# Attention heads' output turned to feature rows by DMA, and the first unit's score maxima computed twice

## What is computed

```python
x = x + 0.5 * ffn0(layernorm(x))      # (W + B @ A) scaled per output: 512 -> 512
x = x + attn0(layernorm(x))           # 32 query heads of 16, 8 key/value heads, rotary, causal
x = x + 0.5 * ffn0(layernorm(x))
x = x + 0.5 * moe(layernorm(x))       # base 512 -> 512, router over 8 experts, top 2, rank-16 LoRA
x = x + attn1(layernorm(x))           # 8 heads of 32, softmax over keys, causal
x = x + 0.5 * moe(layernorm(x))
# attention: softmax(q k^T * scale + causal) v, heads side by side, then @ w_o.T + b_o
```

## Time and profile before

| | |
|---|---|
| Median of three runs | 1358.18 us |
| The profiled execution's own time | 1344.81 us |
| Its span, first to last instruction | 1343.1 us |
| Mean granted TensorE clock | 0.928 of full |
| Busy: PE, DVE, ACT, POOL | 1205.7, 953.5, 671.2, 375.2 us |
| First sequence: A0's first score, its last value product ended | 116.19, 357.79 us |
| Second sequence, the same last value product ended | 1020.49 us |

### The profile page before, as it was taken

One profiled execution on the slowest core, in us unless ns is written; L12 is line 12 of the kernel. 1 busy time (PEld: TensorE's weight loads), 2 busy tenths in 40 slices (PEclk: granted clock), 3 DMA queues, 4 the chain that ended last, 5 costly groups with the idle time before them and its releaser, 6 DMA issues.

```text
span 1343.1 us, 21792 instructions
## 1 busy us (share of the span) xinstructions
PE 1205.7 (90%) x6800; PEld 753.2 (56%) x6800; DVE 953.5 (71%) x2990; ACT 671.2 (50%) x1023; POOL 375.2 (28%) x505
## 2 busy tenths in 40 slices
PE   4998999999899877998879999999988988879988
PEld 1875444443388865444868744444435887744368
DVE  5889889898166676653659798999962667576365
ACT  2621666666655452544436036666665554435542
POOL 0431411122254400114614323122213542002162
PEclk9996899999999997999979858999999999869999
DMA  8374411220010020100140742112200100120001
GB/s 317 120 196 87 125 29 26 57 65 3 1 49 1 1 47 19 55 2 0 63 175 23 189 130 70 26 26 57 66 2 0 50 1 17 32 72 2 1 8 56
DMA packets 37285, 76.20 MB, mean 57 GB/s; under 512 B 5084, under 2 KB 6620, under 8 KB 37036
## 3 DMA queue, kind: packets, MB, share of 16 engines
q1 hardware_dynamic: 37176, 74.82, 19.2%
HBM read 48.98 MB, written 27.08 MB: 57 GB/s over the span
## 4 chain that ended last, share of the span: by engine, by line
PE 64%; DVE 19%; issue 5%; POOL 5%; ACT 5%; DMA 1%; DVEq 0%; SPq 0%; ACTq 0%; POOLq 0%
PE bank L999 16%; PE bank L871 12%; PE bank L779 5%; PE bank L780 5%; PE bank L781 5%; DVE maxes L1208 5%; PE bank L983 4%; PE bank L977 3%; DVE unused L1204 3%; PE bank L765 3%; DVE ops L1152 3%; PE bank L881 2%; POOL x L1484 2%; POOL w_odd L1466 2%; ACT ops L1356 2%
## 5 line engine op out<-in xcount | busy, mean ns | idle before, releaser
L1431 ACT ACTIVATE probs<-bank 128x1024 f32<-128x1024 f32 (+3 forms) x416 | 367.9, 911 | 320.4 <-PE bank L983 220.3
L871 PE MATMUL bank<-ops 48*128 48x512 f32 (+3 forms) x960 | 321.8, 436 | 34.5 <-DVE maxes L1204 17.2
L1204 DVE CUSTOM_DVE_ANT_0 unused<-bank,causal 128x128 bf16<-128x128 f32 (+3 forms) x640 | 279.5, 486 | 47.7 <-PE bank L871 44.1
L1542 POOL TENSOR_SCALAR_AFFINE_SELECT probs<-probs 128x256 f32<-128x256 f32 (+1 forms) x256 | 118.8, 464 | 640.3 <-ACT probs L1431 640.0
L871 PEld LDWEIGHTS bank<-ops 48*128 48x128 f32 (+1 forms) x960 | 163.0, 206 | 218.9 <-DVE maxes L1204 96.0
L999 PE MATMUL bank<-probs,v_mem 128*17 128x512 f32 (+6 forms) x1920 | 252.2, 517 | 6.1 <-ACT heads_raw L1418 5.6
L1208 DVE TENSOR_REDUCE maxes<-bank 128x1 f32<-128x512 f32 x320 | 207.4, 684 | 40.7 <-PE bank L871 39.2
L983 PE MATMUL bank<-ops 50*128 50x512 f32 (+2 forms) x640 | 175.9, 448 | 5.0 <-ACT probs L1431 4.8
L779 PE MATMUL bank<-ops,xT 128*128 128x512 f32 (+1 forms) x288 | 116.2, 403 | 19.6 <-DVE x L1068 11.6
L983 PEld LDWEIGHTS bank<-ops 50*128 50x128 f32 x640 | 86.6, 197 | 57.9 <-ACT probs L1431 29.5
L1473 POOL TENSOR_TENSOR rstd<-var_eps,minus_half 128x1 f32<-128x1 f32 x96 | 52.7, 549 | 215.1 <-DVE var_eps L1046 214.5
(11 more groups left out here) (117 smaller groups left out, 1965.5 us busy)
## 6 DMA issues: line engine op xcount, KB each, us to landing
query_rows_dram<-ops SPq DMA_DIRECT2D x48, 256.0 KB, 3.8
ops<-query_rows_dram SPq DMA_DIRECT2D x64, 192.0 KB, 4.4
w_odd<-staging_wqkv SPq DMA_DIRECT2D x4, 1536.0 KB, 7.3
x<-x_dram SPq DMA_DIRECT2D x16, 256.0 KB, 6.1
ops<-ops SPq DMA_DIRECT2D x16, 256.0 KB, 3.0
out_dram<-x SPq DMA_DIRECT2D x16, 256.0 KB, 2.0
staging_wqkv<-wqkv_dram SPq DMA_DIRECT2D x2, 1536.0 KB, 15.8
key_rows_dram<-ops SPq DMA_DIRECT2D x24, 128.0 KB
```

The costliest lines, as they stand in the source:

```text
L871: last = mm(dst[:, h * w:(h + 1) * w], queries(a, u)[rows, t // 4, hi, t % 4 * P:(t % 4 + 1) * P], keys(a, u, hi)[rows, HALF * kp:HALF * k ...
L1204: V.tensor_tensor_reduce(unused[:, masked % 3, 0:w], part, causal[:, HALF - w:], 1.0, NEG, ALU.add, ALU.max, dst).then_inc(s["max_done"].s ...
L1431: A.activation(probs[:, e % 6, :, 0:cols], scores[:, 2 * (e % 2):2 * (e % 2) + 2, 0:cols], ACT.Exp, scale=a.scale).then_inc(s["exp"].sem, 1)
L1542: G.affine_select(out=p, in_=p, compare_op=ALU.is_ge, fill=0.0, base=0, pattern=pattern, channel_multiplier=-1).then_inc(s["masked"].sem, 1)
```

## The change

1. The "norm" items leave the ring, and WO0 and WO1 lose `turn_x`, `copy_turned` and `turned_lo`. Instead SP stores a chunk's raw heads (256 KB) to a DRAM scratch and loads them back twice, as rows of features with tokens along the free dimension: the values (`head_in`, 128 KB a unit and chunk) and the sum, repeated for each feature of its head (`head_sum`, 128 KB). Two units fill 128 partitions. DVE then takes the reciprocal of the sums (128x512, `inverse_sums`), POOL multiplies and splits into high and low parts (`heads_out`), and the WO products read these (`heads_T`). For the last pair of units DVE does all of it (`last_heads`): chunk 0 at the end of the attention, chunk 1 in tick 3 of the next chain.
2. In the first four steps, and in the ring's items ahead of them from the first not begun in the QKV chain, each score product of a "max" item is issued twice into the same place (`sparse`).
3. `xT` moves into `ops`; MOE_A's weights are loaded after WO0 and split in ticks of tiles 4 to 7 of FFN_B instead of 2 to 5.

```diff
-                if slot == 0:
-                    for c in range(2):
-                        e = s - self.lag - 2 - self.last_step[c]
-                        if e >= 0 and e % ns == 0 and e // ns < self.units:
-                            dst.append(("norm", e // ns, c))
...
+            def load_heads(b, st, u, c):
+                a, s = ATT[st], qs[st]
+                lanes = slice(64 * (u % 2), 64 * (u % 2) + 64)
+                sp.wait_ge(s["raw"].sem, s["raw"].at(b, 2 * u + c + 1))
+                wait(sp, s["staged"][c], b, 32 * u)
+                sp.dma_start(raw_rows[c], heads_raw[:, c, :]).then_inc(s["dumped"][c].sem, 16)
+                sp.wait_ge(s["dumped"][c].sem, s["dumped"][c].at(b, 16 * (u + 1)))
...
+                rows = raw_rows[c].rearrange("(h r) s -> h r s", r=a.head_rows)
+                sp.dma_start(head_in[lanes, c, :], rows[:, 0:a.dim, :]).then_inc(s["staged"][c].sem, 16)
+                sp.dma_start(head_sum[lanes, c, :], rows[:, a.dim:a.dim + 1, :].to_broadcast([a.unit_heads, a.dim, HALF])
+                             ).then_inc(s["staged"][c].sem, 16)
...
                     if u + 1 < a.units:
                         load_shifts(b, QKV0, u + 1, 0)
+                    load_heads(b, QKV0, u, 0)
+                    if u + 1 < a.units:
                         load_shifts(b, QKV0, u + 1, 1)
                     if u + 3 < a.units:
                         sp.wait_ge(s["scored"].sem, s["scored"].at(b, (u + 1) * a.unit_events))
                         load_queries(b, u + 3, 0)
                         load_queries(b, u + 3, 1)
-                    if u in (3, 4):
-                        load_weights(b, FFN_B if u == 3 else MOE_A)
+                    if u == 3:
+                        load_weights(b, FFN_B)
+                    load_heads(b, QKV0, u, 1)
...
                 after(b, WO0)
+                load_weights(b, MOE_A)
...
             def begin(b, st, t):
                 n = product_no(st, t)
-                pe.wait_ge(xT_ready.sem, xT_ready.at(b, TURN_NO[st, t] + 1))
+                if st in WO_ATT:
+                    a, s = WO_ATT[st], qs[QKV0 if st == WO0 else QKV1]
+                    pe.wait_ge(s["out"].sem, s["out"].at(b, 3 * (a.units - 2)))
+                    pe.wait_ge(s["last"].sem, s["last"].at(b, 3 * (t // 4 + 1)))
...
-                    for h, (r, hi) in enumerate(heads_in):
+                    sparse = max(a.begun.values()) <= i < len(a.ring_first) + sum(len(slot) for step in a.ring_at[:4] for slot in step)
+                    for h, (r, hi) in list(enumerate(heads_in)) * (2 if sparse else 1):
...
+                    if c > 0 and i == 3:
+                        last_heads(b, QKV0 if c == 1 else QKV1, 1)
                     if before is not None:
                         epilogue(b, *before)
...
+            def inverse_sums(b, st, k, c):
+                a, s = ATT[st], qs[st]
+                dve.wait_ge(s["staged"][c].sem, s["staged"][c].at(b, 32 * (2 * k + 2)))
+                V.reciprocal(head_sum[:, c, :], head_sum[:, c, :]).then_inc(s["inverse"].sem, 1)
+
+            def last_heads(b, st, c):
...
+                inverse_sums(b, st, k, c)
+                hi, lo = (heads_T(a, part, k)[:, HALF * c:HALF * (c + 1)] for part in range(2))
...
+                V.tensor_tensor(head_out[:, c, :], head_in[:, c, :], head_sum[:, c, :], ALU.mult).then_inc(s["last"].sem, 1)
+                V.tensor_copy(hi, head_out[:, c, :]).then_inc(s["last"].sem, 1)
+                V.tensor_tensor(lo, head_out[:, c, :], hi.bitcast(F32), ALU.subtract).then_inc(s["last"].sem, 1)
...
++                    for i in range(ring_no, upto):
+                        ring_read(b, st, i)
+                    ring_no = upto
+                    u, k_ = divmod(g, len(a.steps))
+                    if u % 2 == 0 and 0 < u < a.units and k_ in (2, 6):
+                        inverse_sums(b, st, u // 2 - 1, k_ // 6)
+                last_heads(b, st, 0)
...
+                        first = 4 if nst == MOE_A else 2
+                        if nb < BATCH and nst not in WO_ATT and first <= t < first + chunks_of[nst]:
+                            split_chunk(nb, nst, t - first)
...
+            def heads_out(b, st, k, c):
...
+                pool.wait_ge(s["inverse"].sem, s["inverse"].at(b, 2 * k + c + 1))
+                G.tensor_tensor(head_out[:, c, :], head_in[:, c, :], head_sum[:, c, :], ALU.mult).then_inc(s["out"].sem, 1)
+                G.tensor_copy(hi, head_out[:, c, :]).then_inc(s["out"].sem, 1)
+                G.tensor_tensor(lo, head_out[:, c, :], hi.bitcast(F32), ALU.subtract).then_inc(s["out"].sem, 1)
...
+                    if u % 2 == 0 and u > 0 and k_ in (4, 7):
+                        heads_out(b, st, u // 2 - 1, k_ // 7)
```

More of the change, by code:

```diff
@@ L411, in all_keys, with heads_T @@
             return ops_flat[:, 16384:20480] if a is A0 else ops_flat[:, 12288:20480]
+        def heads_T(a, part, k):
+            first = ((4096, 5120, 6144, 7168), (8192, 9216, 21504, 14336)) if a is A0 else ((1024, 3072), (4096, 5120))
+            return ops_flat[:, first[part][k]:first[part][k] + SEQ]
         def values(a):
@@ L505, in build @@
             s["raw"] = signal(f"{n}_heads_raw", a.chunks)
-            s["inv"] = signal(f"{n}_inverse_sum", a.chunks)
-            s["normed"] = signal(f"{n}_heads_ready", a.chunks)
+            s["dumped"] = [signal(f"{n}_heads_dumped{c}", 16 * a.units) for c in range(2)]
+            s["staged"] = [signal(f"{n}_heads_staged{c}", 32 * a.units) for c in range(2)]
+            s["inverse"] = signal(f"{n}_inverse_sums", a.units)
+            s["out"] = signal(f"{n}_heads_divided_high_low", 3 * (a.units - 2))
+            s["last"] = signal(f"{n}_last_heads_divided_high_low", 3 * 2)
             qs[st] = s
@@ L830, in product @@
                     pe.wait_ge(w_ready.sem, w_ready.at(b, chunks_before(st + 1)))
-                three_passes(prod[n % 2][:, 0, :], n, weights(st, 0), weights(st, 1)).then_inc(prod_ready.sem, 1)
+                if st in WO_ATT:
+                    x_in = ([heads_T(WO_ATT[st], part, k)[:, t * P:(t + 1) * P] for k in range(chunks_of[st])] for part in range(2))
+                else:
+                    x_in = ([xT[:, n % 2, part, k, :] for k in range(KC)] for part in range(2))
+                three_passes(prod[n % 2][:, 0, :], *x_in, weights(st, 0), weights(st, 1)).then_inc(prod_ready.sem, 1)
             def expert_half(b, st, t, first, between=None):
@@ L838, in expert_half @@
                 cols = slice(0, MOE_HALF) if first else slice(MOE_HALF, MOE_COLS)
-                last = three_passes(prod[n % 2][:, 1 if first else 0, 0:MOE_HALF], n, weights(st, 0)[:, :, cols],
+                x_in = ([xT[:, n % 2, part, k, :] for k in range(KC)] for part in range(2))
+                last = three_passes(prod[n % 2][:, 1 if first else 0, 0:MOE_HALF], *x_in, weights(st, 0)[:, :, cols],
                                     weights(st, 1)[:, :, cols], lora=not first, between=between)
@@ L876, in ring_item @@
                     last = nc.tensor.transpose(dst[0:m, 0:P], shifts[:, n, 0:m].bitcast(F32), identf[:])
-                else:
-                    c = 2 * u + n
-                    pe.wait_ge(s["raw"].sem, s["raw"].at(b, c + 1))
-                    for j in range(4):
-                        last = nc.tensor.transpose(dst[:, j * P:(j + 1) * P],
-                                                   heads_raw[:, c % 2, j * P:(j + 1) * P], identf[:])
                 last.then_inc(s["ring_full"].sem, 1)
@@ L1210, in ring_read @@
                         shift_parts(b, st, u, a.max_banks_of.index(n + 1))
-                elif kind == "shift":
+                else:
                     m = 8 * a.unit_heads
@@ new lines, in attention @@
+            def attention(b, st):
+                a = ATT[st]
+                ring_no = max(a.begun.values())
+                for g, step in [(-1, [a.ring_first])] + list(enumerate(a.ring_at)):
+                    upto = len(a.ring_first) + sum(len(slot) for before in a.ring_at[:g + 1] for slot in before)
+                    for i in range(ring_no, upto):
+                        ring_read(b, st, i)
[4 more added lines that the diff above has]
+                last_heads(b, st, 0)
```

111 lines of the change are left out of this document (52 added, 59 removed).

## The result

The changed kernel took 1433.79 us (median of 4 runs, 1428.13 to 1438.16), beside 1360.18 us for the kernel before on the same chip: a ratio of 1.0589, with an interval of 1.0534 to 1.0643. The prediction had 1359 us and a range up to 1375; it was wrong by far more than its range. The profiled execution after has a span of 1436.4 us; before it was 1343.1. That is 93 us apart where the ratio, which unlike the medians leaves out executions over 1.5% above the fastest of their kernel, gives 80: executions of one kernel differ by that much, and a difference read between two traces carries it.

The account below looks back on a forecast made before the run. A0 was bound by DVE and PE together, A1 by PE, stage ends by dependent steps. Per sequence +7 - 3.3 - 1.5 + 1 - 2.5 = +0.7, +1.4 for two: 1346 us profiled, 1359 as median; range 1339 to 1375.

Parts of the forecast that it names:

- 20.1 us of reciprocals, 3.0 of it filled: A0, units 2, 4 and 6: six reciprocals of 3.35 us, less 3.0 us fitting into DVE's idle time, per sequence.
- nothing, at most +1: A1: DVE's two reciprocals meet 7.4 us of idle time in the unit and cost nothing, at most +1 us.
- units 2, 4 and 6 longer by more than 6 us: A0: sign that the forecast is wrong; those units were to grow by 4 to 5 us.
- My rivals on the clock: Doubled products: clock holds everywhere, -6 for -2.5, 1352 us, chance 0.13; or copies paid at half clock, 1380 us, 0.08.
- DVE becomes the bound of A0: Rival, A0's reciprocals at steps 2 and 6: nothing filled, +10.3 instead of +7, copies' gain halved, 1367 us; chance 0.15.
- I take 5 us ... 6.4 as bounds: Transfers: a chunk's store and two loads through DRAM take 5 us, with 4.0 and 6.4 as bounds.
- -1.5 and +1: Changes per sequence at the starts of WO0 (-1.5 us, bounds -5.2 and +1) and WO1 (+1 us).
- rows land late: Rival, A0: chunk 1's loads pass step 6, each us lost six times; 3 us late costs 18, 1377 us; chance 0.07.
- the 643.9 that I gave: WO1: first product of MOE_B with POOL in DVE's way both times, 3.2 us each; 639.4 without, 641.63 before.
- Predicted -2.5 per sequence: Doubled products: a clock that stays up gains 2.5 us per sequence, bounds -5 and +8.
- the copies paid at half clock: Rival: doubled columns take 16.2 us of PE per attention at 1.2 GHz, DVE hides half; +8 for -2.5, 1380 us; 0.08.
- the -3.3 per sequence: A1: seven normalisations leave before its end, 0.47 us each, -3.3 us per sequence, bounds -4.6 and -2.

Follow-up runs that it names:

- small_in_units: The kernel after, with the reciprocals among the maxima inverting only 32 of their 512 columns: 1376.06 us, ratio 1.0142.
- small_once: small_in_units with the score products made once; the last heads' reciprocals stay whole: 1361.49 us, ratio 1.0032.
- small_all_once: The kernel after, products once, all reciprocals over 32 of 512 columns, the last heads' too: 1342.97 us, ratio 0.9932.
- no_transfers: small_all_once with heads going to DRAM and back only in units 0 and 1 of each attention, later heads' output left out: 1309.53 us, ratio 0.9650.
- once: The kernel after without the doubling of the products: 1420.84 us, ratio 1.0501.
- dummy: The kernel before plus 16 spare 128x512 reciprocals on DVE where the kernel after has those among the maxima: 1423.92 us, ratio 1.0495.
- dummy_half: The kernel before plus the 16 spare reciprocals, over 256 columns each in place of 512: 1389.32 us, ratio 1.0268.
- before_twice: The kernel before with only the doubling of the products, on the same items: 1361.59 us, ratio 1.0078.
- act_inverse: The kernel after, products once, every inverse of the sums made on ScalarE as exp(-ln(s)): 1402.98 us, ratio 1.0312.

## Why the prediction was wrong

By ratios of the kernels above, the 5.9% (80 us of 1358) divide as follows: reciprocals among the maxima 4.5% (after to small_in_units, 61 us), the doubling 1.1% (to small_once, 15 us), the last heads' reciprocals 1.0% (to small_all_once, 14 us), the way through DRAM 2.8% (to no_transfers, 38 us), and against them a gain of 3.5% (48 us) from what the change removes. Each is uncertain by 0.5 to 1.0 points. Two can be had by another way: the reciprocals among the maxima are 4.7% from once to small_once, the doubling is 0.9% from once to the change and 0.8% alone on the kernel before.

**The step that failed first: "20.1 us of reciprocals, 3.0 of it filled".** The 3.35 us were right (3346 ns, the median after). The price was not. It took DVE's own time for what the stage pays, +17.1 per sequence and nothing in A1, 34 us; dummy shows 67 by the ratio. In A1 "nothing, at most +1" per sequence measured 4.8 (158.5 against 148.9 for two). The step added a duration to a ring at an unchanged clock. Dummy's windows say that PE waits less than I charged (1.9 us per reciprocal of 3.35) and then does its products more slowly (4.4 us). The reciprocals alone bring the clock down: nothing else differs between dummy and before. That the waits do it, by leaving PE idle, fits the windows at 200 to 230 us but was not tried by itself, and dummy_half lost 44.0 us of slower products for 3.8 us more of idle time. The prediction had named its own sign: units 2, 4 and 6 longer by more than 6 us. By the copies in the trace after, the six stretches of two units that hold two reciprocals each grew by 5.8 to 14.4 us, although one unit of the two was to lose 1.3. My rivals on the clock had it only as a matter of the doubled products. The rival "DVE becomes the bound of A0" had the right place, but charged at most the reciprocals' own 40 us, where they cost 67.

**"I take 5 us ... 6.4 as bounds" for the transfers.** Measured 7.3 us in A0, 10 in A1 and 12.4 at WO1, outside the bounds. The store was right (1.96 for 2.0); the rows that I went by have neither 128 KB loads of which one is spread from a few rows, nor a store beside loads. In A0's units they are nearly hidden, as I had it: A0 gained 4.3 us when they left. At the starts of WO0 and WO1 I counted them into sums (-1.5 and +1). WO0's came out as far as the traces can tell: what runs from WO0 on, 368.8 us before for two sequences, is 364.0 in once, 367.0 in small_once and 371.5 after, foreseen 3 less. WO1's did not: the last copy and the first product of MOE_B lie 32.4 us apart (660.50 to 692.87) instead of 23.1, +9.3 instead of +1, and the table has 19.7 us more over two sequences. There the transfers and the last reciprocals are the string that the earlier trace rows show with transposes, made longer. The rival "rows land late" named step 6, and in A1 that is where they were late, by 2.5 us; but it looked at A0, and not at the stage starts, where most of the price lies. Two of my sums don't come out, though nothing hangs on them: at WO1, 639.4 and one collision of 3.2 us are 642.6 (+1.0), and two are 645.8, neither the 643.9 that I gave; and the rival on DVE's bound adds up to 1368 and not 1367.

**The doubled products.** Predicted -2.5 per sequence, measured +5 to +7.5 in the mean (0.8 to 1.1% of the whole, over two). The clock did not stay up in the first sequence. Windows after, of the stretches of the earlier trace rows in the first sequence:

```profile
113.50:130.00 16.50, 16.50 (x71) 13.34 (x70) 15.74 (x52) 3.67 (x4) 1.63 (x4) 0.51 0.49 98
130.00:147.00 17.00, 15.86 (x76) 7.38 (x74) 12.87 (x38) 7.32 (x8) 5.90 (x4) 0.50 0.51 174
147.00:180.00 33.00, 32.77 (x191) 13.71 (x188) 25.20 (x87) 20.63 (x27) 10.68 (x17) 0.72 0.31 88
```

The clock is half, and PE, no longer DVE, is the one that is full: 16.50 of 16.50 us. In before_twice the first raw heads come at 151.1 us instead of 143.2. That is the rival of the copies paid at half clock, which I gave 0.08. In the second sequence the clock did stay up for a part, 0.71 and 0.72 after in place of the 0.50 of the earlier trace rows:

```profile
812.00:840.00 28.00, 25.63 (x125) 20.00 (x124) 26.22 (x85) 3.67 (x4) 4.16 (x6) 0.71 0.37 77
840.00:872.00 32.00, 29.03 (x162) 13.54 (x161) 25.44 (x75) 16.34 (x18) 7.71 (x9) 0.72 0.45 150
```

It gained next to nothing: from A1's last copy to the next raw heads before_twice took 186.6 us and before 188.0, but dummy, which doubles nothing, 186.5. Of the 12.6 us between the two traces 7.9 lie ahead of the first raw heads. One thing stays open: A0 of the second sequence took 228.4 us in small_in_units, at a clock of 0.85, and 210.2 in small_once, at 0.95, which differ by the doubling alone; the slow stretches, 33.2 and 38.3 us, lie at units 3 to 5, far behind the doubled items. So the clock can fall in A0 without long reciprocals too.

**What held, and what nearly did.** Units 1 to 3 of A0 are 27.1 us in small_all_once where a full unit took 28.3: 1.2 shorter, foreseen as 1.3. In A1 the first two units are 21.0 us instead of 21.9, as foreseen (1); that the -3.3 per sequence can't be seen in small_once (149.5 against 148.9 for two) is, for 2.5 us a sequence, the late rows of unit 1. WO0's first product came 1.7 us after the last value product (398.7 to 400.4), foreseen within 1: it had to wait for DVE's last operation on chunk 0, which took 1.64 us for 0.69 beside POOL. PE's pause behind tile 2 was 2.3 and what it waited for was DVE, foreseen 3 to 6:

```profile
398.27 0.41 PE L1023 MATMUL bank<-probs,v_mem 128*17 128x128 f32 x8 [0.36 <-POOL probs L1598]
...
400.38 0.51 PE L802 MATMUL bank<-w_odd,ops 128*128 128x512 f32 x1 [1.70 <-issue]
...
412.71 0.47 PE L802 MATMUL bank<-w_odd,ops 128*128 128x512 f32 x1 [2.31 <-DVE x L1096]
```

DVE and POOL collided as feared, but only for chunk 0: in WO1 the multiply took 1.61 us and the cast 1.37 beside POOL's 1.54 and 1.71 (the timeline above), against 0.69 and 0.43 undisturbed, 1.9 us in all; at WO0 chunk 0's three took 0.78, 0.74 and 1.64, 1.3 us more than alone. Chunk 1's, for which I had charged 3.2 us at WO0, took 0.69, 0.43 and 0.69 in all four starts; at 410 us POOL had been idle since 408.8. The Trainium skill, page "SBUF — State Buffer", section "Who interferes with whom", says that a DVE instruction with two SBUF inputs contends with a GpSimd instruction that reads SBUF, and lists casts among the operations that may take the shared pair. This trace agrees with both (1.61 for 0.69, 1.37 for 0.43).

## What to carry to other kernels

Where two engines are coupled by a short ring and both are nearly full, an operation added to one can cost more than its length: here 3.35 us of VectorE cost 4.2 us in the mean over all sixteen, as TensorE's clock fell with it. Test such a price alone, with a spare operation at the place, before building the rest. Look for each transfer's cover place by place: here it was nearly enough in the middle of A0, 2.5 us short in A1, and nothing at a stage's end. And the time of a reciprocal went with its columns here (3.35 us for 512, 0.35 for 32): take it where the sums are compact, not after they are spread.

## What the runs showed of the hardware that I had not expected

- A power on GpSimd over 128x512 took 82 us, 64 times a multiply of that size (1.27 to 1.29 us).
- A reciprocal took 3.35 us for 512 columns, 1.74 for 256, 0.93 for 128, 0.35 for 32 and 0.25 for 16, always over 128 partitions.
- Changing between Ln and Exp on ScalarE loaded a table each time, 1283 ns, 48 times in act_inverse.
- The loads of rows and of spread sums in the kernel after, 128 KB each in both attentions, took 4.8 us in A0 and 7.5 in A1, where a head has 32 rows in place of 16. Why was not tried.
- A store of 256 KB took 1.96 us alone, 4.4 beside two loads of 128 KB, and 7.9 in small_once when it was issued just behind FFN_B's weights (247.36 to 255.21, when SyncE could go on).
